# Transformer layer in one program: shared-expert work of one token group placed ahead of the routed experts, with three small reorderings

## The reference

```
x = x + attention(layernorm(x))                 # 16 blocks of 128 tokens, 16 heads, causal
x = x + cross_attention(layernorm(x), ctx)
flat = layernorm(x)                             # 2048 x 256
shared = swiglu(flat @ w_in.T) @ w_out.T
w_se   = weights of the top 2 of the 4 experts in the better of 2 groups, else 0
h      = swiglu(flat @ w1.T)
routed = sum over e of (h * w_se[:, e:e+1]) @ w2[e].T
return x + shared + routed
```

## Time and profile before

| | us |
|---|---|
| median of 3 timed runs | 825.58 (824.94 to 827.46) |
| the profiled execution | 833.65 |
| its span, first to last instruction | 831.9 |
| PE busy | 789.2 (95%) |
| ACT, DVE, POOL busy | 453.2, 418.5, 280.6 |

### The profile page before, as it was taken

One profiled execution on the slowest core, in us unless ns is written; L12 is line 12 of the kernel. 1 busy time (PEld: TensorE's weight loads), 2 busy tenths in 40 slices (PEclk: granted clock), 3 DMA queues, 4 the chain that ended last, 5 costly groups with the idle time before them and its releaser, 6 DMA issues. The chain is left out here.

```text
span 831.9 us, 16943 instructions
## 1 busy us (share of the span) xinstructions
PE 789.2 (95%) x5859; PEld 668.0 (80%) x5859; DVE 418.5 (50%) x1265; ACT 453.2 (54%) x1475; POOL 280.6 (34%) x302
## 2 busy tenths in 40 slices
PE   7899999999999999999999999999899579999796
PEld 6788888888888887888888888887677369998686
DVE  4556455456456646335453443467586143332347
ACT  4766556656656766566565566567354034453221
POOL 1553224224313644432352343243007700001743
PEclk9999999999999999999999999999999779999889
DMA  7796000000000101000000002010324525662423
GB/s 215 284 399 204 2 0 0 0 0 0 0 0 26 52 26 52 1 27 1 0 25 0 0 0 101 1 26 1 120 84 177 202 101 177 206 198 96 120 76 102
DMA packets 33607, 64.53 MB, mean 78 GB/s; under 512 B 3412, under 2 KB 15060, under 8 KB 32980
## 3 DMA queue, kind: packets, MB, share of 16 engines
q1 hardware_dynamic: 29460, 51.27, 18.4%
q0 software_dynamic: 4096, 12.59, 4.4%
HBM read 38.02 MB, written 30.02 MB: 82 GB/s over the span
## 5 line engine op out<-in xcount | busy, mean ns | idle before, releaser
L438 POOL TENSOR_TENSOR prob<-prob,rsum 128x512 f32<-128x512 f32 x128 | 133.2, 1040 | 353.3 <-DVE rsum L650 353.3
L531 ACT ACTIVATE prob<-psS,nmin 128x128 f32<-128x128 f32 x512 | 180.7, 368 | 50.7 <-PE psT L782 41.3
L629 DVE CUSTOM_DVE_ANT_0 psS<-psS,mask 128x128 f32<-128x128 f32 x256 | 66.5, 323 | 79.9 <-PE psS L771 79.9
L531 ACT ACTIVATION_READ_ACCUMULATOR prob<-psS,nmin 128x1 f32 x512 | 105.3, 206 | 0.0
L632 DVE TENSOR_REDUCE nmin<-psS 128x4 f32<-128x512 f32 x64 | 43.9, 686 | 82.8 <-PE psS L771 82.6
L782 PE MATMUL psT<-ident,prob 128*128 128x128 f32 x512 | 80.4, 279 | 2.7 <-DVE oT_lo L612 2.7
L142 PE MATMUL psA<-wo_lo,oT_hi 128*128 128x256 f32 x256 | 77.1, 301 | 0.0
L771 PE MATMUL psS<-kt,q 64*128 64x128 f32 x1024 | 74.4, 285 | 1.9 <-ACT prob L531 1.9
L1036 POOL DMA_INDIRECT stage<-ys,slot x32 | 33.8, 1055 | 125.3 <-DMA ys<-z 100.1
L509 ACT ACTIVATE v<-psW 128x512 f32<-128x512 f32 x64 | 38.2, 597 | 67.5 <-PE psW L144 67.5
L782 PEld LDWEIGHTS psT<-ident,prob 128*128 128x128 f32 x512 | 58.5, 140 | 19.8 <-issue 3.4
(11 more groups left out here) (284 smaller groups left out, 1949.3 us busy)
## 6 DMA issues: line engine op xcount, KB each, us to landing
hs<-above SPq DMA_DIRECT2D x1, 9984.0 KB, 30.7
stage<-hs SPq DMA_DIRECT2D x39, 256.0 KB, 2.8
ys<-z SPq DMA_DIRECT2D x39, 128.0 KB, 1.7
w_lo<-w_raw SPq DMA_DIRECT2D x4, 1024.0 KB, 8.0
stage<-ctxT SPq DMA_DIRECT2D x4, 512.0 KB, 3.9
out<-xres SPq DMA_DIRECT2D x16, 128.0 KB
xres<-x SPq DMA_DIRECT2D x3, 512.0 KB, 8.3
stage<-wq SPq DMA_DIRECT2D x2, 512.0 KB, 5.7
```

The source lines that it names most:

```text
L438: nc.gpsimd.tensor_tensor(prob[:, r, :], prob[:, r, :], rsum[:, r].unsqueeze(2).broadcast_to([P, TPG, P]), ALU.mult).then_inc(prob_done, 1)
L531: e = nc.scalar.activation(prob[:, n, :], flat(psS[:])[:, n * P:(n + 1) * P], ACT.Exp, bias=nmin[:, n:n + 1], scale=-1.0, accum_out=psums[ ...
L629: m = nc.vector.tensor_tensor_reduce(sc, sc, mask[:], 1.0, LARGE, ALU.add, ALU.min, nmin[:, i * TPG + n:i * TPG + n + 1])
```

## The change

Four things are changed.

1. `BEHIND` becomes the index of S10. The units S00 to S03 and `shared_out(0)` go in front of the experts; `shared_out(3)` now stands behind S00. ScalarE and VectorE follow with their parts. The table of adds behind the experts is re-made: two tiles at S11, two at S20 (where before one each), and none during group 0.
2. The register read of the expert's address stands in front of the transposes of the tile two ahead, instead of behind them.
3. In the last group's attention steps, the statistics of the second and third layer norm move behind the reciprocals and copies of their step on VectorE, and in the last step TensorE's output projection moves behind the transposes and the weighted values.
4. Of the four loads of the first token group, ScalarE issues the second and the fourth, ahead of its table load; SyncE issued all four before.

```
-                for t in range(TPG):
+                for t in range(0, TPG, 2):
                     sp.dma_start(xres[:, t, :], xv_[0][:, t, :]).then_inc(x_first[t], 16)
...
+                for t in range(1, TPG, 2):
+                    act.dma_start(xres[:, t, :], xv_[0][:, t, :]).then_inc(x_first[t], 16)
                 act.preload_act_table(ACT.Exp)
...
-                        if j == LN_AT or 0 < n < 3:
+                        if j == LN_AT:
                             dve.wait_ge(res_done, NGRP + ORDER[n] + 2)
                             ln_stats(dve, L0 + n, ORDER[n])
...
+                    if after == 2 and j in (LN_AT + 1, PAIRS - 2):
+                        n = 1 if j == LN_AT + 1 else 2
+                        dve.wait_ge(res_done, NGRP + ORDER[n] + 2)
+                        ln_stats(dve, L0 + n, ORDER[n])
...
-                        out_project((j - 2) % PAIRS, j % 2)
+                        if after < 2 or j < PAIRS - 1:
+                            out_project((j - 2) % PAIRS, j % 2)
...
                         weighted_values(s, (j - 1) % PAIRS)
+                    if after == 2 and j == PAIRS - 1:
+                        out_project(j - 2, j % 2)
...
-            BEHIND = UNITS.index("S00")
+            BEHIND = UNITS.index("S10")
...
-                for name, n in (("S01", 0), ("S02", 1), ("S03", 1), ("S10", 1), ("S11", 1), ("S12", 1), ("S13", 1), ("S20", 1), ("S21", 2), ("S22", 1),
-                                ("S23", 1)):
+                for name, n in (("S11", 2), ("S12", 1), ("S13", 1), ("S20", 2), ("S21", 2), ("S22", 1), ("S23", 1)):
...
-                    if name in ("S10", "S20"):
-                        add_shared(int(name[1]) - 1)
+                    if name == "S20":
+                        add_shared(1)
...
                 for m in range(HT):
                     unit(f"S3{m}")
+                unit("S00")
                 shared_out(3)
+                for m in range(1, HT):
+                    unit(f"S0{m}")
+                shared_out(0)
...
                 for i in range(NT):
+                    offset = offset_of(i)
                     if i + 2 < NT:
                         turn(i + 2)
-                    expert(i)
+                    expert(i, offset)
...
                 for name in UNITS[BEHIND:]:
                     unit(name)
-                    if name == "S10":
-                        shared_out(0)
```

More of the change, by code:

```diff
@@ L494, in _ @@
             def _(act):
+                xv_ = x.rearrange("(g t p) d -> g p t d", p=P, t=TPG)
+                for t in range(1, TPG, 2):
+                    act.dma_start(xres[:, t, :], xv_[0][:, t, :]).then_inc(x_first[t], 16)
                 act.preload_act_table(ACT.Exp)
@@ L1089, in _ @@
                 unit(UNITS.index("S30"))
-                for m in range(HT - 1):
-                    unit(UNITS.index(f"S3{m}") + 1)
-                    split(f"S3{m}")
-                split("S33")
-                w2_hi_part(6)
-                w2_hi_part(7)
+                for u in range(UNITS.index("S30") + 1, BEHIND):
+                    unit(u)
+                    split(UNITS[u - 1])
+                    if UNITS[u - 1] == "S33":
+                        w2_hi_part(6)
+                        w2_hi_part(7)
+                split(UNITS[BEHIND - 1])
                 def expert_hi(i):
@@ L1346, in _ @@
                 unit(UNITS.index("S30"))
-                for m in range(HT - 1):
-                    unit(UNITS.index(f"S3{m}") + 1)
-                    split(f"S3{m}")
-                split("S33")
-                w2_lo_part(6)
-                w2_lo_part(7)
-                add_shared(3)
+                for u in range(UNITS.index("S30") + 1, BEHIND):
+                    unit(u)
+                    if UNITS[u] == "S01":
+                        add_shared(3)
+                    split(UNITS[u - 1])
+                    if UNITS[u - 1] == "S33":
+                        w2_lo_part(6)
+                        w2_lo_part(7)
+                split(UNITS[BEHIND - 1])
+                add_shared(0)
                 for i in range(NT):
@@ L1458, in turn, with offset_of, expert @@
                     tr.then_inc(hT_mm, 1)
-                def expert(i):
-                    offset = pe.value_load(offsets[0:1, i:i + 1], min_val=0, max_val=(NE - 1) * D)
+                def offset_of(i):
+                    return pe.value_load(offsets[0:1, i:i + 1], min_val=0, max_val=(NE - 1) * D)
+                def expert(i, offset):
                     pe.wait_ge(hT_lo, i + 1)
```

## The result

| us | before | after |
|---|---|---|
| median of the timed runs | 825.61 (824.94 to 827.46, 4 runs) | 835.31 (830.41 to 837.78, 4 runs) |
| the profiled execution | 833.65 | 830.41 |
| its span | 831.9 | 828.6 |
| first transposes of an expert tile | 684.89 | 692.80 |
| first matmul behind the experts | 763.98 | 770.60 |

The ratio of after to before is 1.0083 (95% interval 1.0055 to 1.0111): 0.8% slower, where 822.1 was forecast with a range of 818 to 831. Of all executions in this document one, of `after_fourth`, fell into a slower state (953.59 us at a mean granted clock of 0.752) and is left out of its ratio.

A forecast was written before the change was run, and what follows sets the result against it. TensorE was taken as the bound nearly everywhere, slowed around the experts by late-seen completions during GpSimd's indirect DMAs. Terms -0.6 - 1.4 + 17.0 + 0 - 18.5 = -3.5 us took the median from 825.58 to 822.1, range 818.0 to 831.0.

The forecast's parts named there:

- What bounds the kernel: TensorE busy nearly everywhere; time to win lies before and behind the experts, where GpSimd issues indirect DMAs.
- The lag: After some 12 us or longer of GpSimd issuing indirect DMAs, other engines see late what TensorE finishes.
- Group 0 taken out of the tail, -18.5: From TensorE's first matmul behind the experts to the end: 67.9 us falls to 49.4, bound by the gathers.
- the first rival: Late completions persist behind the experts as GpSimd runs through 24 gathers: 58.7 instead of 49.4 us, 831.4 us total; chance 0.23.
- second mark: Behind the experts, a sign of the forecast being wrong: `shared_out(1)` takes 10 us or more.
- Group 0 in front, +17.0: Before the experts: four shared units (11.3 us) and `shared_out(0)` (5.8) cost 17.0 us, none covered by idle time.
- Sum, and its carrying to the median: Whole kernel: terms total -3.5 us, taking the profiled execution to 830.2 and the median from 825.58 to 822.1.
- The lag as a thing of the profiled run: Timed runs lack late completions: about 9 of 17 us cost before the experts, 8 won behind; 822.6 us; chance 0.15.
- attention: Last group's reordered attention steps: gaps of TensorE at 572.66 and 585.39 shrink, -1.4 us (-1.6 to 0).
- start: Loads at the start: two fewer on SyncE ahead of the first weight, -0.6 us (-0.9 to 0).
- The read: In the experts, the register read moved before the transposes: 0 us (-2.2 to +3); rival gaining 2.2, 819.9 us, chance 0.07.

The follow-up runs named there:

- after_again: The changed kernel, unchanged, measured again: 835.38 us, ratio 1.0082 to the kernel before.
- after_fourth: The changed kernel, unchanged, measured again where no completions came late: 812.84 us, ratio 0.9991 to the kernel before.
- after_third: The changed kernel, unchanged, measured again where completions came late: 838.14 us, ratio 1.0099 to the kernel before.
- move_only: The kernel before with only group 0's four shared units and their output moved in front of the experts: 837.72 us, ratio 1.0081 to before.
- before_again: The kernel before, unchanged, measured again: 830.25 us, ratio 1.0001 to before.
- rest_only: The changed kernel without the move of group 0, keeping only the small edits: 829.01 us, ratio 0.9969 to the kernel before.

## Why the prediction was wrong, point by point

**What bounds the kernel: right, and not carried through.** The lag was read correctly from the earlier trace rows and tied to GpSimd's run. Plain loads and pacing both bear this out, with the limit on the plain loads named above.

**Group 0 taken out of the tail, -18.5: the step that failed.** The sum let the tail go by the gathers, 49.4 us, with 9 us of slack for TensorE. Measured: 58.0, 57.1 and 59.2 in three traces, so -9.9 where -18.5 was put. The lateness did not stay within the slack; it reached 16.9 us, and behind it TensorE's granted clock was 0.50 for a while. That is the first rival, which had 58.7. Its reason was right too: three tiles more are added before the next shared output, so GpSimd isn't stopped by its buffers after 18 gathers. It is stopped after 28 in the first trace of after, and after exactly the 24 that the rival had in `after_again`, `after_third` and `move_only`; this row of `after_third` is its 25th gather:

```profile
820.36 1.09 POOL L1046 DMA_INDIRECT stage<-ys,slot  x1 [8.53 <-DVE xres L1324]
```

Its second mark, `shared_out(1)` at 10 us or more, is missing in the first trace (784.7 to 790.5) and there in others, since the lateness has two forms. In `after_third` the matmuls of the projection themselves crawl, 17.0 us for 48, and VectorE's add of their result comes later still:

```profile
791.80 0.28 PE L142 MATMUL psA<-wout_lo,hid_hi 128*128 128x256 f32 x1
...
807.38 0.37 PE L143 MATMUL psA<-wout_hi,hid_hi 128*128 128x256 f32 x1 [1.03 <-issue]
...
808.80 0.58 PE L142 MATMUL psT<-z_lo,wq_hi 128*128 128x512 f32 x1 [0.84 <-issue]
```
```profile
814.74 1.29 DVE L1313 TENSOR_TENSOR xres<-psA,xres 128x512 f32<-128x512 f32 x2 [16.24 <-remote]
```

In the first trace of after they start on time, and only what waits on them, on ScalarE and VectorE, is late. With plain loads the step is worth some -16 us. With real gathers and no lateness the tail is 51.9 us: the gathers came 1.38 us apart instead of 1.306 (762.72 to 805.55), and 6.5 us follow the start of the last. The 1.306 was small already against its own rows: from the 1st to the 18th gather are 17 spacings, (788.99 - 766.48) / 17 = 1.324, not 23.5 / 18. But the step is worth only -5.7 us there, not -18.5, since the 67.9 us from which it was taken hold the lateness of before; without that the tail is 57.6 to begin with.

**Group 0 in front, +17.0: right in size, wrong to read off one trace.** 17.5 us of work were added. What they cost depends on what TensorE would have done otherwise: 15.6 us with late completions (rest_only to after_again), 7.3 without. The step said that no idle time covers the work; that holds only as long as the lateness itself keeps TensorE behind the loads.

**Sum, and its carrying to the median: wrong.** The -3.5 was made against an execution 8.1 us above the median, and carried over as it was. In the trace of before the front had lost more than usual (first transposes at 684.9, against 681.4 in `before_again`), so the next front looked cheap beside it. The traces of after and before differ by -3.2, the medians by +9.7, and the traced execution of after was the shortest of its four. The base was the place where the error could have been seen: the prediction noted the 8.1 us and did not ask what both kernels would do in an execution without it. The Trainium skill ("Runtime: NRT & Kernel Launch", section "The ~15µs preamble/postamble breakdown") puts a gap of about 6.2 us, the same for every kernel, between a profile's total and the time of an execution. The runs here don't record that total; each execution's time exceeds its span by about 1.75 us, and profiled executions lie among the timed ones (830.07 in 827.95 to 837.74), so the 8.1 us are not that gap.

**The first rival (831.4, chance 0.23)** had the right mechanism and was still 4 us short of the median (1 us by the ratio), because it was added to the same base: 825.6 + 5.8. From two traces of one measurement: 15.6 in front, less 10.8 in the tail, less 1.2 over the experts is +3.6 between the spans of rest_only and after_again, +6.4 between their medians. The traced execution of after_again, 832.46, is the shortest of its twelve and 2.9 us under their median, that of rest_only lies at its median: that accounts for the other 2.8 us, though one trace of each doesn't tell where the longer executions spend them.

**The lag as a thing of the profiled run (822.6)** was put the wrong way round. By their times the lateness is in the timed runs too, or in none of them: it belongs to the measurement, not to the profiling. Where it is absent, the rival's terms were fair (front +9, tail -8; measured +7.3 and -5.7), and the ratio is 0.9991 instead of its 0.996.

**The small terms: attention right, start not seen.** One pair of traces misleads here: by 595 us after is 1.0 us ahead of before, with -0.4 at the start (TensorE's first projection at 10.77 us instead of 11.21), and that looks like half of the forecast 2.0. Over all traces the first projection comes at 10.63 to 11.39 us in the six with the old loads and at 10.62 to 12.39 us in the fourteen with the new ones, so the -0.6 put for the loads shows nowhere. Nor does it later: at 152 us the old loads stand at 150.9 to 153.5 us and the new ones at 151.7 to 154.8 (the last psT transposes of one step, 151.36 in before, 151.85 in after). The reordered steps, from the transposes in front of them (563.06) to the first unit H0 (595.82), take 31.21 to 31.24 us in all fourteen, and in the six others 32.76 or 32.77 three times and 34.28 to 34.30 three times:

```profile
563.06 1.04 PE L192 MATMUL psW<-ident,z 128*128 128x128 f32 x8
...
595.82 0.47 PE L142 MATMUL psT<-w_lo,z_hi 128*128 128x512 f32 x1 [0.32 <-PEq L322]
```
```profile
563.56 1.03 PE L192 MATMUL psW<-ident,z 128*128 128x128 f32 x8
...
594.80 0.47 PE L142 MATMUL psT<-w_lo,z_hi 128*128 128x512 f32 x1 [0.32 <-PEq L322]
```

So the reordering is worth 1.5 us, forecast 1.4, and 3.1 in half of the executions: there TensorE's granted clock fell behind the wait of 1.85 us (0.52 in `before_again`, 586.1 to 589.3 us), which it never did behind the 0.88 us left. From that transpose to these steps all twenty traces take 411.7 us; what varies from trace to trace is the first 152 us, and in the one pair that hid a third of the gain. The read: 0 forecast, -0.14% measured, at the edge of the interval. All the small edits together are worth 0.3% with late completions (2.6 us by the ratio, 0.8 by the medians) and 0.5% without (4.2 and 3.9 us), beside the 2.0 of the sum.

## What to carry to other kernels

Work moved in front of a phase costs only what isn't covered by that phase's own wait, and work taken out of a tail gains only down to the next limit: price both at the two places where the trace could look different, not only where it does. When a profiled execution is far from the median, make the sum once for each kind of execution before carrying it over. And where one engine issues a long unbroken row of indirect DMAs, tie every few of them to the progress of the engine that the rest waits for; here it cost nothing where nothing was late, and won 1.0% by itself (2% in the changed kernel) where something was. Before believing a term of 1 us read off two traces, look how far the unchanged stretches of these traces differ.

## What the runs showed of the hardware that was not expected

- During a run of indirect DMAs on GpSimd, what TensorE has finished is seen by ScalarE and VectorE up to 16.9 us late (in the gathers; 16.0 in the scatters of before), or its matmuls crawl with 0.3 to 1.1 us of idle time in front of each, or both. It begins 10 to 18 us into the run, and the last late Silus start 3 to 6 us after the run's last DMA. Whether the matmuls end late or only the notice of them comes late can't be told, since their ends are modelled.
- It is there in every trace of one measurement or in none, and, to judge by the times, in all its executions: before took 825.6 to 829.9 us in four measurements and 813.0 and 813.1 in two, 2% apart, and the ranges don't meet (824.94 or more, 815.74 or less). The last two measurements were made on a chip of the same number, one with it and one without, so it isn't simply the chip, as the expectation of `after_third` had it. The scatter's packets take the same time in both: from 625 to 665 us 2375 packets fill 51.1% of the 16 DMA engines in before and 2211 fill 47.6% in `after_fourth`, 138 ns each. What switches it is open.
- One thing goes with it in the traces: a time from issue to landing of GpSimd's indirect gathers is shown in all six without lateness (medians of 2.8 to 3.0 us) and in none of the twelve with it; here `after_third`, then `after_fourth`. Whether that is a cause or only a gap in the records isn't shown.

```profile
stage<-ys,slot POOLq DMA_INDIRECT x32
```
```profile
stage<-ys,slot POOLq DMA_INDIRECT x32, 2.9
```

- The lower level of the clock (granted 0.5, that is 1.2 of 2.4 GHz) came behind every wait of TensorE of 3.5 to 10.3 us in the traces, behind some of its waits of 1.85 to 2.7 us and not behind others, and also with the crawling, where no gap is longer than 1.1 us. In the tail of `after_again` TensorE looks busy, with 16 matmuls in 10 us (columns as the earlier trace rows):

```profile
800.00:810.00 10.00, 8.25 (x16) 4.43 (x16) 0.00 (x0) 0.00 (x0) 6.13 (x7) 0.50 0.32 95
```
